# Picking each expert's 64 tokens: drawing the highest of three sequences early, in partition quarters, and merging them with the fourth

## The chip, the cores and the metric

The kernel runs on one core of a Trainium2 chip. The metric is the device time of one execution in microseconds (us). A core has five engines that run their own instruction lists and wait for each other through semaphores: TensorE (PE, matrix products and transposes, into PSUM), VectorE (DVE), ScalarE (ACT), GpSimd (POOL) and SyncE (SP, which here only issues DMAs).

## What is computed

The reference is a decoder of two layers on x of 4 sequences x 256 tokens x 128. Layer 0 is local attention, then self and cross attention, then a mixture of 16 experts; layer 1 is a recurrence, cross attention and a second mixture. The change concerns the choice of tokens in layer 0's mixture:

```
logits = xn @ router_weight.T + router_bias      # 1024 tokens x 16 experts
probs = jax.nn.softmax(logits, axis=-1)
_, idx = jax.lax.top_k(logits.T, top_k)          # top_k = 64 tokens of 1024, for each expert
xe = xn[idx]
...
output = jnp.zeros((n_tokens, d)).at[flat_idx].add(contrib)
```

Each expert takes the 64 tokens with its highest logits out of all four sequences; of equal logits the earlier token goes first.

## The kernel before

**The attention pipeline.** Layer 0's attention is `attention_pipeline` with 12 jobs: 4 local ones, then self and cross attention of each sequence in turn. Job n begins its core work at slot 16n, and every engine walks through the slots 0 to 249 in order and does in each what falls into it: a unit of row maxima (PE scores, DVE `nmax` at L1093), one head of scores and exponentials (PE L866, ACT L974), a quarter of the products with V (PE L907), and the job's end steps: transpose (L820), division (`y`, L1036 to L1043), output product (L772), residual sum and statistics (`z`, L1052 to L1060), 1/std on POOL (L753), and norm (L1069 writes `m.x[1]`, the tokens for the experts, with semaphore `xs_ready`; L1073 writes `m.x[2]`). The last job, number 11, is the cross attention of sequence 3: its 16 heads are slots 214 to 229, its division is in DVE's slot 237, its sum in slot 241, its norm in slot 243. Waits only follow data: a slot has no fixed length, and an engine may be slots ahead of another.

**Side work.** `expert_choice` hangs its own steps into the slots (`sync`, `gpsimd`, `tensor`, `scalar`, `vector`, each called at the head of a slot) and continues after the last slot (`sync_on`, `gpsimd_on`, ...). A side step that uses the shared PSUM bank M1 (bank 7) has its turn in the list `part.uses`, and waits until the use before it has been read.

**The choice.** Before the change PE transposes the tokens of sequences 0 and 1 in slot 230 and of sequence 2 in slot 234 (L1266), ACT multiplies them by the norm weight (L1375), PE makes the logits [16 x 1024] in three groups (L1272), ACT adds the bias (L1380); the last group (sequence 3) follows after the last slot. Then DVE takes the eight highest of all 1024 columns (MAX8, L1436) and overwrites them with a constant (MATCH_REPLACE8, L1438), eight times, marks the places taken (L1440), counts them along the row (a scan, L1441), and so has `posb`, the slot number of each token in each expert or 0 (L1442). PE turns `posb` (L1304), DVE copies it (L1448) and compares it with 1 to 64 for each of 8 token tiles (L1451), which makes the one-hot matrices `onehot`; PE gathers the tokens with them (L1312, 48 products of 512 columns), and the experts follow. SP writes `posb` to DRAM and reads it back 16 times, spread over partitions, for the scatter (L1214, L1217). POOL splits the normed tokens `xn` into three bf16 terms (L1247 to L1250). `keep_warm` runs 18 products that nobody reads (L504) on PE before `posb` is there.

Of the kernel before, what the change touches and what calls it, by code (L numbers as in the profile page):

```python
# [14 lines left out]
BF16 = mybir.dt.bfloat16  # L15
# [9 lines left out]
P = 128  # L25
# [452 lines left out]
GROUPS = ((0, 512), (512, 768), (768, 1024))  # L478
S_ROUTER, S_NORM_COL, S_OPEN = 140, 226, 230
# [657 lines left out]
def expert_choice(nc, m, dram, ctx, rec):  # L1137


    part = Core()  # L1140
# [12 lines left out]
    logits = m.xres[0:E0, :, :].rearrange("p t d -> p (t d)")  # L1153
    work = m.x[0][0:E0, :, :].rearrange("p t d -> p (t d)")
    top8 = sb("top8", [E0, 8])
    ones = sb("ones", [E0, TOK], BF16)
    posb = sb("posb", [E0, TOK], BF16)
    taken = m.xT[0][0:E0, 0:TOK // 2].bitcast(BF16)
    count = m.xT[0][0:E0, TOK // 2:TOK].bitcast(BF16)
# [14 lines left out]
    wr = sb("wr", [P, E0])  # L1174
    rb = sb("rb", [E0, 1])
# [16 lines left out]
        "h_mm", "h_in", "h_act", "y_mm", "ygl_ready", "out_mm")]  # L1192
    var_ready, rms_ready, ex_in, rounds, turning = sem("var_ready"), sem("rms_ready"), sem("ex_in"), sem("rounds"), sem("turning")
    x2, x3 = m.x[2], m.x[0]
    out_rows = lambda i: (B[2], B[3], B[6], B[7])[i // 2][:, (i % 2) * D:(i % 2 + 1) * D]
    part.uses = [(S_NORM_COL, "norm_col", 0), (S_OPEN, "xs", 0)]

    def sync(sp, slot):
        if slot == S_ROUTER:
            sp.dma_start(wr[:, :], dram["routerT"]).then_inc(r_in, 16)  # L1200
            sp.dma_start(rb[:, :], dram["router_b"]).then_inc(r_in, 16)
            sp.dma_start(b1[:, :, :], dram["fc1b"]).then_inc(w_in, 16)
            for half in range(2):
                src = dram["fc2b"].rearrange("(r o) d -> o r d", o=2)[half:half + 1, :, :]
                sp.dma_start(b2[64 * half:64 * half + 64, :, :], src.to_broadcast([64, PAIRS, D])).then_inc(w_in, 16)

    def sync_on(sp):
        sp.wait_ge(part.pv_done, 12 * BATCH)
        sp.dma_start(fc2, dram["fc2T"]).then_inc(fc2_in, 16)
        sp.wait_ge(r_in, 32)  # L1210
# [3 lines left out]
        sp.dma_start(pos_rows, posb[:, :]).then_inc(pos_out, 16)  # L1214
        sp.wait_ge(pos_out, 16)
# [10 lines left out]
    def gpsimd(pool, slot):  # L1226
        if slot != S_OPEN:
            return
        g = nc.gpsimd
        link = chain(pool, pchain, pool_count)  # L1230
# [9 lines left out]
        pool.wait_ge(const, 3)  # L1240

    def gpsimd_on(pool):
        g = nc.gpsimd
        link = chain(pool, pchain, pool_count)
        pool.wait_ge(xnT_mm, 2)
        pool.wait_ge(xn_ready, 2)
# [5 lines left out]
        pool.wait_ge(lg_in, 3)  # L1252
# [11 lines left out]
    def turned(pe, bank, first, tiles, done):  # L1264
        for i in tiles:
# [3 lines left out]
    def routed(pe, bank, k):  # L1269
        pe.wait_ge(xnT_in, k + 1)  # L1270
        lo, hi = GROUPS[k]
        nc.tensor.matmul(bank[0:E0, 0:hi - lo], wr[:, :], xnT[:, lo:hi], start=True, stop=True).then_inc(lg_mm, 1)  # L1272

    def tensor(pe, slot):
# [4 lines left out]
        if slot == S_OPEN:  # L1279
            pe.wait_ge(part.m1_read, part.m1_no["xs", 0])  # L1280
            pe.wait_ge(part.xs_ready, 2)
            turned(pe, M1, 0, range(0, 4), part.m1_full)
        if slot == S_OPEN + 4:
            pe.wait_ge(part.xs_ready, 3)
            turned(pe, B[1], 4, range(4, 6), xnT_mm)
        if slot == S_OPEN + 7:
            pe.wait_ge(r_in, 32)
            routed(pe, B[0], 0)
        if slot == S_OPEN + 9:
            routed(pe, B[2], 1)  # L1290

    def tensor_on(pe):
        t = nc.tensor
        pe.wait_ge(part.xs_ready, 4)
        turned(pe, B[3], 6, range(6, 8), xnT_mm)
        routed(pe, B[1], 2)
        pe.wait_ge(lg_in, 3)
        for i in range(TILES):
            t.transpose(B[4][:, i * E0:(i + 1) * E0], logits[:, i * P:(i + 1) * P], m.ident[0:E0, 0:E0]).then_inc(lgT_mm, 1)
        pe.wait_ge(rounds, CAP // 8 - 1)  # L1300
# [72 lines left out]
    def weighed_by_norm(act, bank, k):  # L1373
        lo, hi = GROUPS[k]
        return nc.scalar.activation(xnT[:, lo:hi], bank[:, 0:hi - lo], ACT.Copy, scale=norm_col[:, :])  # L1375

    def with_bias(act, bank, k):
        act.wait_ge(lg_mm, k + 1)
        lo, hi = GROUPS[k]
        nc.scalar.activation(logits[:, lo:hi], bank[0:E0, 0:hi - lo], ACT.Identity, bias=rb[:, :]).then_inc(lg_in, 1)  # L1380

    def scalar(act, slot):
# [5 lines left out]
        if slot == S_OPEN + 1:  # L1388
            act.wait_ge(part.m1_full, part.m1_no["xs", 0] + 1)
            weighed_by_norm(act, M1, 0).then_inc(part.m1_read, 1)  # L1390
            act.wait_ge(part.m1_read, part.m1_no["xs", 0] + 1)
            s.sem_inc(xnT_in, 1)
        if slot == S_OPEN + 5:
            act.wait_ge(xnT_mm, 1)
            weighed_by_norm(act, B[1], 1).then_inc(xnT_in, 1)
# [878 lines left out]
```

## Time and profile before

| what | value |
|---|---|
| three timed runs | 572.04, 574.46 (median), 580.11 us |
| the profiled execution | 571.62 us |
| its span in the trace | 569.9 us |
| mean granted TensorE clock | 0.955 of full speed |
| busy: PE, DVE, ACT, POOL | 470.7, 372.7, 223.3, 186.6 us |

The span runs from the first to the last instruction in the trace; 1.72 us of the execution lie outside it. Rows name a line of the kernel, an engine and an operation, output<-input with their sizes (partitions x columns), and a count. An idle time in square brackets is that of the engine just before the row, with what ended it.

### The profile page before, as it was taken

What the parts mean: (1) busy time and instruction counts of PE and PEld (TensorE: products, weight loads), DVE (VectorE), ACT (ScalarE), POOL (GpSimd) and SP (SyncE); (2) the same over time, 40 slices, a digit from 0 to 9 for tenths busy, and PEclk for the clock granted to TensorE, in tenths of its full rate; (3) what the DMA queues carried; (4) which work ended last, traced back from release to release, by engine and by line L of the source; (5) the groups of instructions that cost most, each with busy time, mean ns of one, the idle gap of its engine ahead of it and who ended that gap; (6) DMA issues with size and microseconds to landing.
All of it is one profiled execution on the core that took longest, in us unless ns stands there. A gap on an engine that the chain in (4) does not pass through costs nothing. (4 is left out here: it accounts for less than half of the span.)

```text
span 569.9 us, 10425 instructions
## 1 busy us (share of the span) xinstructions
PE 470.7 (83%) x3785; PEld 232.4 (41%) x3832; DVE 372.7 (65%) x868; ACT 223.3 (39%) x451; POOL 186.6 (33%) x310
## 2 busy tenths in 40 slices
PE   3899899988979889885069998697799888999993
PEld 2445444433334333332026986254233333444441
DVE  7555766877677677823996474854478784466574
ACT  1313444445754656673002122332114667624220
POOL 7752639467344471333200005720542100000000
PEclk9999999989998999998579999899699999999998
DMA  7230103054441220007013040000321100250700
GB/s 240 72 96 12 49 2 104 21 178 138 144 106 49 58 56 3 2 3 294 0 39 112 2 168 2 0 1 1 85 56 37 48 3 3 67 157 2 222 18 19
DMA packets 26900, 38.03 MB, mean 67 GB/s; under 512 B 3649, under 2 KB 19521, under 8 KB 26465
## 3 DMA queue, kind: packets, MB, share of 16 engines
q1 hardware_dynamic: 26848, 37.36, 21.8%
q8 instruction: 31, 0.51, 0.4%
q14 instruction: 21, 0.16, 0.1%
HBM read 23.91 MB, written 0.59 MB: 43 GB/s over the span
## 5 line engine op out<-in xcount | busy, mean ns | idle before, releaser
L1093 DVE TENSOR_REDUCE nmax<-bank 128x2 f32<-128x512 f32 (+2 forms) x240 | 144.4, 624 | 79.6 <-PE bank L862 37.9
L974 ACT ACTIVATE arena<-bank 128x512 f32<-128x512 f32 (+2 forms) x256 | 130.9, 526 | 122.6 <-PE bank L866 84.7
L862 PE MATMUL bank<-arena 62*128 62x256 bf16 (+2 forms) x512 | 86.0, 257 | 11.8 <-DVE nmax L1093 5.0
L504 PE MATMUL bank<-causal_qk,identb 128*128 128x512 bf16 x232 | 71.1, 402 | 26.1 <-DVE moe_top L1436 16.0
L866 PE MATMUL bank<-arena 64*128 64x256 bf16 (+2 forms) x512 | 85.8, 256 | 2.2 <-ACT arena L974 1.5
L907 PE MATMUL bank<-arena 128*32 128x256 f32 (+4 forms) x1088 | 73.0, 347 | 9.3 <-POOL arena L729 2.8
L862 PEld LDWEIGHTS bank<-arena 62*128 62x128 bf16 x512 | 29.8, 94 | 77.5 <-issue 46.6
L504 PEld LDWEIGHTS bank<-causal_qk,identb 128*128 128x128 bf16 x275 | 23.8, 104 | 55.7 <-DVE moe_top L1436 15.7
L729 POOL TENSOR_SCALAR_AFFINE_SELECT arena<-arena 128x256 f32<-128x256 f32 x64 | 25.6, 410 | 48.8 <-ACT arena L974 48.0
L866 PEld LDWEIGHTS bank<-arena 64*128 64x128 bf16 x512 | 30.3, 94 | 16.6 <-ACT arena L974 6.5
L907 PEld LDWEIGHTS bank<-arena 128*32 128x32 f32 x1088 | 21.4, 109 | 34.2 <-issue 19.1
L688 POOL TENSOR_TENSOR arena<-qk,arena 128x512 bf16<-128x512 f32 x15 | 17.4, 1157 | 52.2 <-ACT arena L936 52.2
L518 POOL TENSOR_SCALAR veps<-mv 128x2 f32<-128x2 f32 x8 | 1.5, 193 | 91.0 <-DVE mv L1541 73.8
L2085 ACT ACTIVATE arena<-bank 128x512 f32<-128x512 f32 x24 | 14.3, 597 | 40.6 <-PE bank L2067 40.6
L2095 DVE TENSOR_TENSOR arena<-bank,arena 128x512 f32<-128x512 f32 x24 | 16.5, 689 | 16.4 <-ACT arena L2085 16.1
L2072 PE MATMUL bank<-arena,fcw 128*128 128x512 f32 x48 | 24.5, 594 | 0.4 <-DVE arena L2101 0.4
L2066 PE MATMUL bank<-xT,fcw 128*128 128x512 f32 x48 | 24.7, 596 | 0.0
L2067 PE MATMUL bank<-xT,fcw 128*128 128x512 f32 x48 | 24.5, 592 | 0.0
L751 POOL TENSOR_SCALAR veps<-mv 128x2 f32<-128x2 f32 x12 | 2.7, 225 | 64.1 <-DVE mv L1060 63.8
L784 PE MATMUL bank<-xT,h 128*128 128x256 f32 x32 | 11.8, 453 | 11.6 <-DVE h L400 9.9
L2137 POOL TENSOR_TENSOR rstd<-veps,eps 128x4 f32<-128x4 f32 x2 | 2.0, 1008 | 55.3 <-DVE veps L2178 55.3
L928 ACT ACTIVATE qk<-bank,qs_cols 128x256 f32<-128x256 f32 x16 | 7.5, 470 | 29.9 <-PE bank L785 29.9
(296 smaller groups left out, 813.5 us busy)
## 6 DMA issues: line engine op xcount, KB each, us to landing
arena<-arena SPq DMA_DIRECT2D x96, 128.0 KB, 2.4
fcw<-in_fc1T SPq DMA_DIRECT2D x16, 256.0 KB, 3.3
arena<-in_fc2T SPq DMA_DIRECT2D x1, 4096.0 KB, 12.5
arena<-comb_rows SPq DMA_DIRECT2D x16, 256.0 KB, 4.3
fcw<-in_last SPq DMA_DIRECT2D x1, 2304.0 KB, 8.3
arena<-pos_rows SPq DMA_DIRECT2D x16, 128.0 KB, 3.0
arena<-comb_rows SPq DMA_DIRECT2D x16, 128.0 KB, 4.3
w<-in_w SPq DMA_DIRECT2D x1, 1216.0 KB, 6.1
```

Source lines behind the costliest of these rows:

```text
L504: nc.tensor.matmul(bank[:, :], m.identb[:, :], m.causal_qk[:, 0:4, :], start=True, stop=True)
L688: g.tensor_tensor(parts[:, 4], src, parts[:, 0], ALU.subtract).then_inc(split, 1)
L729: g.affine_select(out=part, in_=part, compare_op=ALU.is_ge, fill=0.0, base=0, pattern=[[0, 2], [1, P]], channel_multiplier=-1).then_inc(ke ...
L862: mins = t.matmul(mout[:, i, :], stack_rows(m, nm, h0 + i, 0, MAX_ROWS)[:, qt * P:(qt + 1) * P], stack_rows(m, nm, h0 + i, 1, MAX_ROWS)[:, ...
L866: sins = t.matmul(sout[i], stack_rows(m, nh, h, 1, SCORE_ROWS)[:, i * P:(i + 1) * P], stack_rows(m, nh, h, 0, SCORE_ROWS)[:, spans[i][0]:s ...
L907: ins = t.matmul(PV[n % len(PV)][32 * i:32 * i + 32, lo + a:lo + b], m.vaug[n % 4][:, k, h, :], m.prob[h % 8][:, o0 + a - q0:o0 + b - q0], ...
L974: s.activation(m.prob[h % 8][:, 0:w], score_bank(n, h)[:, 0:w], ACT.Exp).then_inc(exps, 1)
L1093: v.tensor_reduce(m.nmax[n % 2][:, qt, h0:h0 + nh], MX[c % NMX][:, 0:nh * (k1 - k0)].rearrange("p (h k) -> p h k", h=nh), AX.X, ALU.max, n ...
L2066: t.matmul(B[k][:, :], self.w1[:, f * P:(f + 1) * P], xT, start=True, stop=True)
L2067: t.matmul(B[k + 1][:, :], self.w3[:, f * P:(f + 1) * P], xT, start=True, stop=True).then_inc(self.hg_mm, 1)
L2072: self.nc.tensor.matmul(self.acc[c][:, :], self.w2[:, f, :], self.hid[u % 2], start=(f == 0), stop=(f == HT - 1)).then_inc(self.o_mm, 1)
L2095: v.tensor_tensor(self.sil[u % 2], self.m.bank[2 * (u % 2) + 1][:, :], self.sil[u % 2], ALU.mult).then_inc(self.gs_in, 1)
```

## The change

The logits of the four sequences lie one under another: sequence b in partitions 32b to 32b+15, 256 columns each. They are made by four products, each with the router's weights padded by zeros to 32 columns. The transposes and logits of sequences 0 and 1 are moved to slots 196 and 199, those of sequence 2 to slots 216 and 219, all in bank M1; the norm column goes from slot 226 to 186. In its slots 222 to 229 DVE draws, in eight rounds, the 64 highest of each of the first three sequences at once (96 partitions x 256 columns). In slot 230 it copies the three lists side by side ([16 x 192]); the 64 highest of these are drawn in eight rounds: two in slot 238, one in 239, two in 242, three after the last slot. When the logits of sequence 3 are there, they are copied beside that list ([16 x 320]), and eight rounds give the 64th highest value of each expert. DVE then compares all logits ([128 x 256]) with it, "greater" and "equal", and counts both by a scan; two small products on PE with 0/1 matrices (`before_it`, `of_expert`, made on POOL in slot 230) give each partition the counts of the sequences before it; from these come `posb`, now [128 x 256]. The product that makes `xn` moves from DVE (L1420) to POOL, as one instruction after the last norm. `keep_warm` starts after the fourth of the last eight rounds instead of the seventh of before.

```diff
+QUARTER = P // BATCH
+EARLY = QUARTER * (BATCH - 1)
+S_ROUTER, S_NORM_COL, S_OPEN = 140, 186, 226
+S_TURN, S_ROUTED = ((196, 0, 4), (216, 4, 6)), ((199, (0, 1)), (219, (2,)))
+S_DRAW, S_GATHER, S_MERGE = 222, 230, (238, 238, 239, 242, 242)
...
+    logits = flat[:, 0:SEQ]
+    pooled = flat[0:E0, SEQ:2 * SEQ + CAP]
+    three = flat[0:E0, 2 * SEQ + CAP:3 * SEQ]
+    lists = flat[0:EARLY, 3 * SEQ + CAP:3 * SEQ + 2 * CAP]
+    highest = flat[0:E0, 3 * SEQ + 2 * CAP:3 * SEQ + 3 * CAP]
...
+            sp.wait_ge(padded, 2)
+            sp.dma_start(wr[:, 0:E0], dram["routerT"]).then_inc(r_in, 16)
+            for b in range(BATCH):
+                sp.dma_start(rb[QUARTER * b:QUARTER * b + E0, :], dram["router_b"]).then_inc(r_in, 16)
...
-        sp.dma_start(pos_rows, posb[:, :]).then_inc(pos_out, 16)
-        sp.wait_ge(pos_out, 16)
+        for b in range(BATCH):
+            sp.dma_start(pos_rows[:, b * SEQ:(b + 1) * SEQ], posb[QUARTER * b:QUARTER * b + E0, :]).then_inc(pos_out, 16)
+        sp.wait_ge(pos_out, 16 * BATCH)
...
+        g.memset(fact[:, :], 0.0).then_inc(const, 1)
+        for matrix, quarters in ((before_it, range(1, BATCH)), (of_expert, range(1 - BATCH, BATCH))):
+            link(g.memset(matrix[:, :], 0.0))
+            for q in quarters:
+                link(g.affine_select(out=matrix[:, :], in_=matrix[:, :], compare_op=ALU.not_equal, fill=1.0,
+                                     base=QUARTER * q, pattern=[[-1, P]], channel_multiplier=1))
+        g.sem_inc(const, 1)
+        pool.wait_ge(const, 5)
...
+        pool.wait_ge(part.xs_ready, BATCH)
+        pool.wait_ge(part.pv_done, 9 * BATCH)
+        link(g.tensor_tensor(xn, m.x[1][:, :, :], row(m, "moe_norm").unsqueeze(1).broadcast_to([P, TILES, D]), ALU.mult))
+        pool.wait_ge(xnT_mm, 1)
...
+        for k, (at, lo, hi) in enumerate(S_TURN):
+            if slot == at:
+                pe.wait_ge(part.m1_read, part.m1_no["xs", k])
+                pe.wait_ge(part.xs_ready, hi // QT)
+                turned(M1, lo, hi, part.m1_full)
+        for k, (at, sequences) in enumerate(S_ROUTED):
+            if slot == at:
+                pe.wait_ge(r_in, 16 + 16 * BATCH)
+                pe.wait_ge(part.m1_read, part.m1_no["routed", k])
+                routed(M1, sequences, part.m1_full)
...
+        pe.wait_ge(drawn, 1)
         keep_warm(nc, m, B[7], F_ROUTE)
+        pe.wait_ge(counted, 1)
+        pe.wait_ge(const, 5)
+        t.matmul(B[2][:, 0:2], before_it[:, :], ranks[:, :, SEQ - 1], start=True, stop=False, skip_group_check=True)
+        t.matmul(B[2][:, 1:2], of_expert[:, :], ranks[:, 0, SEQ - 1:SEQ], start=False, stop=True, skip_group_check=True).then_inc(count_mm, 1)
...
+        for k, (at, lo, hi) in enumerate(S_TURN):
+            if slot == at + 1:
+                act.wait_ge(part.m1_full, part.m1_no["xs", k] + 1)
+                weighed_by_norm(M1, lo, hi).then_inc(part.m1_read, 1)
+        for k, (at, sequences) in enumerate(S_ROUTED):
+            if slot == at + 1:
+                act.wait_ge(r_in, 16 + 16 * BATCH)
+                act.wait_ge(part.m1_full, part.m1_no["routed", k] + 1)
+                with_bias(M1, sequences).then_inc(part.m1_read, 1)
...
+    def draw(link, source, out, spent, i):
+        v = nc.vector
+        eight = out[:, 8 * i:8 * i + 8]
+        link(v.max(eight, spent if i else source))
+        if i < CAP // 8 - 1:
+            link(v.match_replace(out=spent, in_to_replace=eight, in_values=spent if i else source, imm_value=TAKEN))
...
+        if slot == S_DRAW:
+            dve.wait_ge(part.m1_read, part.m1_no["routed", 1] + 1)
+        if S_DRAW <= slot < S_DRAW + CAP // 8:
+            draw(link, logits[0:EARLY, :], lists, work, slot - S_DRAW)
+        if slot == S_GATHER:
+            for b in range(BATCH - 1):
+                link(v.tensor_copy(three[:, CAP * b:CAP * (b + 1)], lists[QUARTER * b:QUARTER * b + E0, :]))
+        for i, at in enumerate(S_MERGE):
+            if slot == at:
+                draw(link, three, pooled[:, 0:CAP], three, i)
...
+        for i in range(len(S_MERGE), CAP // 8):
+            draw(link, three, pooled[:, 0:CAP], three, i)
+        dve.wait_ge(lg_in, 1)
+        link(v.tensor_copy(pooled[:, CAP:CAP + SEQ], logits[EARLY:EARLY + E0, :]))
...
+            draw(link, pooled, highest, pooled, i)
+            if i == CAP // 16 - 1:
+                v.sem_inc(drawn, 1)
+        dve.wait_ge(const, 5)
+        for b in range(BATCH):
+            link(v.tensor_copy(fact[QUARTER * b:QUARTER * b + E0, 0:1], highest[:, CAP - 1:CAP]))
+        for k, op in enumerate((ALU.is_gt, ALU.is_equal)):
+            link(v.tensor_scalar(compared[:, k, :], logits, fact[:, 0:1], None, op))
+        for k in range(2):
+            link(v.tensor_tensor_scan(ranks[:, k, :], ones[:, :], compared[:, k, :], 0.0, ALU.mult, ALU.add))
+        v.sem_inc(counted, 1)
+        dve.wait_ge(count_mm, 1)
+        link(v.tensor_copy(fact[:, 1:3], B[2][:, 0:2]))
+        for k in range(2):
+            link(v.scalar_tensor_tensor(out=placed[:, k, :], in0=ranks[:, k, :], scalar=fact[:, 1 + k:2 + k], in1=compared[:, k, :],
+                                        op0=ALU.add, op1=ALU.mult))
+        link(v.tensor_scalar(kept, placed[:, 1, :], float(CAP), None, ALU.is_le))
+        link(v.tensor_tensor(kept, kept, placed[:, 1, :], ALU.mult))
+        v.tensor_tensor(posb[:, :], placed[:, 0, :], kept, ALU.add).then_inc(pos_ready, 1)
```

## Rows read from the trace of the kernel before

**Rows 1.** The waits from 240 to 330 us: who waited for whom, total us, times, longest.

```profile
ACT moe_gate L1408 <- DVE moe_lgT L1446: 24.8, 1, 24.8
POOL veps L518 <- DVE mv L1060: 16.0, 1, 16.0
```

**Rows 2.** DVE's timeline, 228 to 312 us: start us, us, what.

```profile
259.26 0.36 DVE L1036 RECIPROCAL rden<-bank 128x32 f32<-128x32 f32 x1 [7.46 <-PE bank L820]
...
262.53 0.42 DVE L1052 TENSOR_TENSOR z<-bank,xres 128x256 f32<-128x256 f32 x1 [1.93 <-PE bank L772]
...
266.25 0.60 DVE L1073 TENSOR_SCALAR x<-z,mv,rstd 128x128 f32<-128x128 f32 x2
...
269.21 1.22 DVE L1436 MAX8 moe_top<-xres 16x8 f32<-16x1024 f32 x1 [2.03 <-ACT xres L1380]
...
292.71 0.68 DVE L1442 TENSOR_TENSOR moe_posb<-xT 16x1024 bf16<-16x1024 bf16 x1
...
294.16 9.17 DVE L1451 TENSOR_TENSOR arena<-moe_iota_s,moe_posT 128x1024 bf16<-128x1024 bf16 x8
```

**Rows 3.** PE's timeline, 254 to 308 us.

```profile
255.97 0.66 PE L1266 MATMUL bank<-ident,x 128*128 128x128 f32 x4
...
259.15 1.03 PE L1272 MATMUL bank<-xT,moe_wr 128*16 128x512 f32 x2
...
286.23 5.72 PE L504 MATMUL bank<-causal_qk,identb 128*128 128x512 bf16 x17 [15.97 <-DVE moe_top L1436]
293.44 0.35 PE L1304 MATMUL bank<-identb,moe_posb 16*128 16x16 bf16 x8 [1.49 <-DVE moe_posb L1442]
295.53 12.21 PE L1312 MATMUL bank<-arena 128*128 128x512 bf16 x47 [1.73 <-DVE arena L1451]
```

**Rows 4.** DVE's instruction groups by form, 268 to 295 us: busy us, mean ns | idle.

```profile
L1436 DVE MAX8 moe_top<-x 16x8 f32<-16x1024 f32 x7 | 8.5, 1216 | 0.2
L1438 DVE MATCH_REPLACE8 x<-moe_top,x 16x1024 f32<-16x1024 f32 x7 | 8.4, 1196 | 0.0
L1441 DVE TENSOR_TENSOR_SCAN xT<-moe_ones,xT 16x1024 bf16<-16x1024 bf16 x1 | 2.3, 2278 | 0.0
...
L1440 DVE TENSOR_SCALAR xT<-x 16x1024 bf16<-16x1024 f32 x1 | 0.7, 682 | 0.0
L1442 DVE TENSOR_TENSOR moe_posb<-xT 16x1024 bf16<-16x1024 bf16 x1 | 0.7, 678 | 0.0
L1438 DVE MATCH_VALUE_LOAD x<-moe_top,x 16x8 f32 x7 | 0.6, 79 | 0.2
```

**Rows 5.** The shortest group that MAX8 has in the kernel, and the scan of 256 and the three-operand operation of 512 columns, by form.

```profile
L1787 DVE SCALAR_TENSOR_TENSOR arena<-bank,cols,hid 128x512 f32<-128x512 f32 x8 | 6.0, 751 | 10.4 <-ACT hid L1712 10.3
...
L1762 DVE TENSOR_TENSOR_SCAN arena<-arena,cols 128x256 f32<-128x256 f32 x4 | 2.8, 738 | 0.1
...
L1924 DVE MAX8 top_top<-top_lg 128x8 f32<-128x8 f32 x8 | 1.3, 167 | 0.2
```

**Rows 6.** Timelines of all engines at 170 us, of DVE at 240 and of POOL at 268 us.

```profile
170.26 1.16 POOL L696 TENSOR_TENSOR rem<-qk,arena 128x512 f32<-128x512 f32 x1
...
170.77 0.68 DVE L1082 CAST nml<-nmax 128x32 bf16<-128x32 f32 x1
...
240.19 0.18 DVE L1082 CAST nml<-nmax 128x32 bf16<-128x32 f32 x1
...
268.46 2.12 POOL L1248 TENSOR_TENSOR x<-arena 128x1024 f32<-128x1024 f32 x1
```

**Rows 7.** Busy time 228 to 246 us (PE, PEld, DVE, ACT, POOL; PE clock, DMA share, GB/s).

```profile
228.00:246.00 18.00, 15.04 (x170) 6.17 (x172) 13.12 (x29) 11.26 (x25) 8.13 (x22) 1.00 0.01 4
```

**Rows 8.** The waits of SP's queue from 150 to 215 us.

```profile
SPq L649 <- ACT arena L936: 20.7, 3, 8.6
```

**Rows 9.** Stretches of 1 us, with the granted PE clock third from the end.

```profile
296.00:297.00 1.00, 1.00 (x6) 0.45 (x5) 1.00 (x2) 0.00 (x0) 0.00 (x0) 0.93 0.23 90
...
300.00:301.00 1.00, 1.00 (x5) 0.44 (x4) 1.00 (x2) 0.00 (x0) 0.00 (x0) 0.86 0.56 201
```

More of the change, by code:

```diff
@@ L1152, in expert_choice @@
     xnT = m.xT[0]
[L1153 to L1159, printed above, removed]
+    flat = m.hid[:, :, :].rearrange("p a c -> p (a c)")
+    logits = flat[:, 0:SEQ]
[3 more added lines that the diff above has]
+    highest = flat[0:E0, 3 * SEQ + 2 * CAP:3 * SEQ + 3 * CAP]
+    work = m.qk32[0][0:EARLY, 0:SEQ]
+    ones = sb("ones", [P, SEQ], BF16)
+    posb = sb("posb", [P, SEQ], BF16)
+    compared = m.xT[0][:, 0:SEQ].bitcast(BF16).rearrange("p (k t) -> p k t", k=2)
+    ranks = m.xT[0][:, SEQ:2 * SEQ].bitcast(BF16).rearrange("p (k t) -> p k t", k=2)
+    placed = m.xT[0][:, 2 * SEQ:3 * SEQ].bitcast(BF16).rearrange("p (k t) -> p k t", k=2)
+    kept = m.xT[0][:, 3 * SEQ:3 * SEQ + SEQ // 2].bitcast(BF16)
+    fact = sb("fact", [P, 3])
+    before_it = sb("before_it", [P, P], BF16)
+    of_expert = sb("of_expert", [P, P], BF16)
     posT = sb("posT", [P, TILES, E0], BF16)
@@ L1251, in gpsimd_on @@
         pool.wait_ge(xnl_ready, 1)
-        pool.wait_ge(lg_in, 3)
+        pool.wait_ge(lg_in, 1)
+        pool.wait_ge(part.x1_ready, 2 * BATCH)
         pool.wait_ge(fc2_in, 16)
@@ L1262, in gpsimd_on, with turned, routed @@
         rec.gpsimd_on(pool)
-    def turned(pe, bank, first, tiles, done):
-        for i in tiles:
+    def turned(bank, first, last, done):
+        for i in range(first, last):
             ins = nc.tensor.transpose(bank[:, (i - first) * P:(i - first + 1) * P], m.x[1][:, i, :], m.ident[:, :])
         ins.then_inc(done, 1)
[L1269 to L1272, printed above, removed]
+    def routed(bank, sequences, done):
+        for b in sequences:
+            ins = nc.tensor.matmul(bank[QUARTER * b:QUARTER * (b + 1), 0:SEQ], wr[:, :], xnT[:, b * SEQ:(b + 1) * SEQ], start=True, stop=True)
+        ins.then_inc(done, 1)
     def tensor(pe, slot):
@@ L1278, in tensor @@
             t.transpose(M1[:, 0:P], row(m, "moe_norm"), m.ident[:, :]).then_inc(part.m1_full, 1)
[L1279 to L1288, printed above, removed]
@@ L1292, in tensor_on @@
     def tensor_on(pe):
         t = nc.tensor
[L1294 to L1300, printed above, removed]
+        pe.wait_ge(part.xs_ready, BATCH)
+        turned(B[3], TILES - QT, TILES, xnT_mm)
+        pe.wait_ge(xnT_in, 1)
@@ L1302, in tensor_on @@
         pe.wait_ge(pos_ready, 1)
-        for i in range(TILES):
-            t.transpose(B[5][:, i * E0 // 2:(i + 1) * E0 // 2].bitcast(BF16), posb[:, i * P:(i + 1) * P],
-                        m.identb[0:E0, 0:E0]).then_inc(posT_mm, 1)
+        for q in range(QT):
+            t.transpose(B[5][:, q * P // 2:(q + 1) * P // 2].bitcast(BF16), posb[:, q * P:(q + 1) * P],
+                        m.identb[:, :]).then_inc(posT_mm, 1)
         pe.wait_ge(xnl_ready, 1)
@@ L1371, in tensor_on, with weighed_by_norm, with_bias @@
         rec.tensor_on(pe)
[L1373 to L1380, printed above, removed]
+    def weighed_by_norm(bank, lo, hi):
+        return nc.scalar.activation(xnT[:, lo * P:hi * P], bank[:, 0:(hi - lo) * P], ACT.Copy, scale=norm_col[:, :])
+    def with_bias(bank, sequences):
+        lanes = slice(QUARTER * sequences[0], QUARTER * (sequences[-1] + 1))
+        return nc.scalar.activation(logits[lanes, :], bank[lanes, 0:SEQ], ACT.Identity, bias=rb[lanes, :])
     def scalar(act, slot):
```

84 lines of the change are left out of this document (30 added, 54 removed).

## Prediction, written before the changed kernel was run

> **What bounds the kernel now.** I read the waits around 240 to 330 us first, then the timelines of the engines there. The chain of waits that ended last begins only at 397 us, so it says nothing of this place. ACT waits 24.8 us for the logits' exponentials [rows 1], because DVE alone works: from 269.21 to 294.16 it goes without a pause through eight rounds, the marking, the scan and the product, and only then starts the one-hot matrices [rows 2]. PE idles 15.97 us in it [rows 3]. Ahead of it the order is: sum `z` at 262.53 (waits for PE's output product), norm, transposes and logits of sequence 3, first MAX8 at 269.21 after 2.03 us for ACT's bias [rows 2]. Nothing after it is tied to a time of its own: `posb` at 293.39 (292.71 + 0.68) releases PE, DVE and SP's round trip alike, and the gather products run from 295.53 for 12.21 us [rows 3]. So what DVE saves between 269.2 and 293.4 comes off the end nearly one for one, unless PE's clock takes some of it back.
>
> **What is removed.** One round is 1216 + 79 + 1196 = 2491 ns of instructions [rows 4]; the eight rounds, marking, scan and product take 293.39 - 269.21 = 24.18 us, of which the rounds are 20.47 (289.68 is what is left ahead of 682 + 2278 + 678 ns and their gaps), so 69 ns of a round are gaps.
>
> **What the last eight rounds cost.** They work on 320 columns. MAX8 takes 167 ns for 8 columns [rows 5] and 1216 for 1024, so 1.03 ns a column: 0.49 us for 320. MATCH_REPLACE8 at the same slope: 0.47 (1196 less 704 columns). A round is 0.49 + 0.08 + 0.46 + 0.07 = 1.09 us; seven of them and a last MAX8 are 8.2 us. That the partitions don't matter is seen in MAX8's 128 partitions at 167 ns, near the fixed part of the 16-partition form.
>
> **The rest of the new chain on DVE.** Four copies of one column, 0.20 us each with its wait (bounds 0.1 and 0.25): 0.8. Two comparisons of 256 columns with a scalar from memory: the marking took 682 for 1024 [rows 4], so about 0.35 (0.28 to 0.42), 0.75 with gaps. Two scans of 256: 738 ns each [rows 5], 1.55. Two products on PE and back: no row has such a pair. The eight small transposes took 0.35 and started 0.05 after `posb` [rows 3]; I take 0.5 (0.35 to 0.8), and 0.2 for reading the counts. Two three-operand operations: 751 for 512 columns [rows 5], so 0.46 each, 1.0 together (0.7 to 1.1). The last three, from the product's 678 for 1024 [rows 4], are 0.22 + 0.28 + 0.28 with gaps 0.85. Sum 5.65, bounds 4.7 to 6.5. With the rounds: 13.8 us from the copied logits to `posb`, where 24.18 stand now. The turn of `posb`, the maximum and `posT` are the same work in another layout (two transposes of 128 partitions for eight small ones); I cost them at nothing, at most 0.3.
>
> **The early draws.** On 96 x 256 a round is 0.42 + 0.08 + 0.40 + 0.07 = 0.97 us, together 7.3, and 0.6 for the three copies. DVE stood idle for 7.46 us up to the division of job 11 at 259.26 [rows 2], from 251.80 that is, and what it did just before, the first part of the `xn` product, goes. From about 251 (an estimate, with ACT's bias of slot 220 ahead of it) the draws end at 258.9, so they fit with 0.4 us to spare. Without that cover each us over costs one.
>
> **The merges.** On 192 columns a round is 0.35 + 0.08 + 0.34 + 0.07 = 0.84 us. The three of slots 238 and 239 follow the division, which ends at 260.6 (262.53 - 1.93): 2.5 us to 263.1, where `z` stood ready at 262.53 [rows 2]. Cost 0.6 us, on the path: the logits come at 269.8 instead of 269.2. The two of slot 242 (1.7) lie in the wait for POOL's 1/std. The last three, 2.1 us, lie in the 2.03 us in which DVE waits for sequence 3's logits.
>
> **POOL and the port.** The `xn` product on 1024 columns now starts when the last L1069 is done, with DVE's two L1073 still under way; its like took 2.12 us [rows 6]. The rows show what such a meeting does: DVE's cast of 32 columns, 0.18 us when POOL is idle, took 0.68 at 170.77 and ended at 171.45, as POOL's product did at 171.42 [rows 6]. MAX8 and MATCH_REPLACE8 are not held: all eight are 1216 and 1196 ns [rows 4], and POOL's product ran from 268.46. So I expect: POOL takes its turn between the two L1073; the second ends some 2.1 us late (267.2 + 2.1); three merges (2.1) end at 271.4; the copy of sequence 3's logits then meets POOL's next product and gets through at about 272.8 instead of 270.1 (269.8 + 0.3). The other end is 270.6, if DVE comes first at L1073 and the copy waits only for the rest of a shorter POOL cast. I take 272.8, as that cast did.
>
> The Trainium skill (SBUF — State Buffer, Who interferes with whom) says the same of the pair of ports which the two engines share: whoever issues first keeps it for its whole instruction; copies and tensor-scalar forms ask for it, an instruction with one input outside those modes does not. It speaks against moving `xn` to POOL; by it the time is the forecast below, without it 2.2 us less.
>
> **What moves into the attention loop.** PE's six transposes and the logits of three sequences leave slots 230 to 239, where they lay beside ACT's and DVE's steps, and go to slots 196 to 219. The four transposes took 0.66 and 512 columns of logits 1.03 [rows 3]: 2.5 us of PE altogether, and some 2 us of ACT, most of it into a stretch in which PE is busy 15.04 of 18 us, DVE 13.12 and ACT 11.26 [rows 7]. If the idle 2.96 us absorb them, 0; if PE is always the last, 2.6. I take 1.2, near the middle, since no engine is full there. The semaphores are old by then (sequence 2's norm is over before slot 216). The norm column is moved unchanged.
>
> **POOL's and SP's other steps.** POOL builds its matrices between 248 and 264, where it waits 16.0 us [rows 1], and nobody needs them before 279; cost nothing, though a delay of its 1/std would be paid in full. SP waits in slot 140 for two memsets and issues three more small DMAs, with the stack transfers behind it. In those SP waits for ACT anyhow, 20.7 us in three times [rows 8]; against waits of that size three issues cost nothing. The four writes of `posb` instead of one are 1 us more of SP; the first columns are needed after nine us of one-hot matrices, so nothing.
>
> **PE's clock.** At 1.2 GHz a product of 512 columns lasts twice as long. In the gather stage the clock stood at half from the end of the slice 296-297 to early in 300-301 [rows 9], some 3.3 us, about 5 after the reader-less products had ended at 291.95 [rows 3]. Now these start at about 278.4 (272.8 + 1.2 + four rounds) and end by 284.3; the gather starts 2.14 us after `posb`, as now, at about 289.9. The gap is 5.6 us, where it was 3.6 (295.53 - 291.95), so the clock is likely down when the gather starts. What a cold start costs: 48 products less 1.65 us of half clock are 10.56 us, 0.22 each, so the 17 reader-less ones would be 3.7 us and took 5.72 [rows 3], 2 us lost instead of 1.65. Cost 0.3.
>
> **Sum.** `posb`: 272.8 + 13.8 + 1.2 = 287.8 instead of 293.39, so 5.6 earlier, less 0.3: 5.3 us. The 0.6 of the merges stands in the 269.8. Against the profiled execution's 571.62: 566.3. That execution is the fastest of four; the median of all four (571.62, 572.04, 574.46, 580.11) is 573.25, or 1.6 above it, so I forecast **567.9 us**.
>
> **The rivals.**
> - A, everything fits better: POOL holds nothing (2.2), the loop absorbs the moved work (1.2) and the clock stays up in the gather (1.9 with the 0.3): 562.6. For it: DVE's instructions are queued ahead of POOL's. Against: the cast of rows 6. Chance 0.2.
> - B, the other end: the loop pays 2.6, the chain 6.5 instead of 5.65, and the early draws run 1 us over the division's time: 3.2 us less gained, 571.1. Chance 0.2.
> - C, slower than before: the loop is in lockstep. PE waits in its four new places for ACT's reads, with the scores and maxima of both running jobs queued behind it, and DVE and ACT wait for those; if each place costs over 1.6 us ((5.3 + 1.2) / 4), the change loses. At 2.5 us each it is 10 less the 1.2 counted: 576.7. Against: the bank was read slots before each of these places, and ACT is busy 11.26 of 18 us [rows 7]. Chance 0.05.
> - D, the port: what is held isn't one instruction each but also the comparisons and `z`; the reverse of A: another 2 us, 569.9. POOL is through with its five instructions by 276, before the comparisons. Chance 0.05.
>
> The forecast itself (565 to 570) has 0.5. Two per cent (11.5 us) are about what a measurement of this kernel can tell from no change: faster by over 2% needs all of A and a low median, 0.1; slower by over 2% needs C at full price, 0.02; within 2%, 0.88. The range, 561.5 to 572.5, takes in A and B.
>
> **What the changed profile would show.** MAX8 on 16x320 of 0.48 to 0.50 us, eight times; draws over before the last division; `z` 0.6 us later against the division; the second L1073 near 2 us late, ending with POOL's product; 13 to 15 us from the copy to `posb`; the slots 196 to 220 longer by 0 to 2.6; the clock's half-speed stretch at the gather's start. The prediction is wrong if DVE's draws start so late that they pass the division's time, if the four column copies or the trip to PE cost over 1 us more than stated, or if the clock stays down through the gather (48 products, up to 8 us more).

## The result: 572.4 us, 3.3 us less by the ratio, where 5.3 to 6.9 were forecast

| | before | changed |
|---|---|---|
| median of 13 runs each | 574.75 us (571.52 to 580.11) | 572.43 us (568.88 to 577.35) |
| ratio of the runs | | 0.9943, 95% interval 0.9918 to 0.9968 |
| profiled execution, time / span | 571.62 / 569.9 us | 577.35 / 575.5 us |

The medians are 2.3 us apart; the ratio, which weighs all 13 runs of each, says 3.3 us less, between 1.8 and 4.7. Within 2% was given a chance of 0.88. The forecast, 567.9, asked for 5.35 us less than the median that it started from, and for 6.85 less than this one. In the ratios of the experiments below, runs more than 1.5% above the fastest of their kernel are left out, which concerns one of six and two of twelve in the two kernels whose only addition is products ahead of the gather. The profiled execution of the changed kernel is the longest of its 13, so whole spans can't be compared. What can are stretches of it that begin and end with the same instruction. First DVE's timeline:

```profile
227.71 0.36 DVE L1039 RECIPROCAL rden<-bank 128x32 f32<-128x32 f32 x1 [0.41 <-PE bank L823]
243.48 0.35 DVE L1039 RECIPROCAL rden<-bank 128x32 f32<-128x32 f32 x1
257.34 0.36 DVE L1039 RECIPROCAL rden<-bank 128x32 f32<-128x32 f32 x1 [4.60 <-PE bank L823]
...
265.65 0.62 DVE L1465 COPY hid<-hid 16x64 f32<-16x64 f32 x3
266.86 0.36 DVE L1039 RECIPROCAL rden<-bank 128x32 f32<-128x32 f32 x1 [0.60 <-PE bank L823]
270.83 0.42 DVE L1055 TENSOR_TENSOR z<-bank,xres 128x256 f32<-128x256 f32 x1
274.08 0.60 DVE L1072 TENSOR_SCALAR x<-z,mv,rstd 128x128 f32<-128x128 f32 x2 [0.39 <-DVE hid L1454]
274.60 2.64 DVE L1076 TENSOR_SCALAR x<-z,mv,rstd 128x128 f32<-128x128 f32 x2
279.19 1.42 DVE L1476 COPY hid<-hid 16x256 f32<-16x256 f32 x1
280.64 0.48 DVE L1452 MAX8 hid<-hid 16x8 f32<-16x320 f32 x1
294.00 0.29 DVE L1496 TENSOR_TENSOR moe_posb<-xT 128x256 bf16<-128x256 bf16 x1
294.98 9.17 DVE L1508 TENSOR_TENSOR arena<-moe_iota_s,moe_posT 128x1024 bf16<-128x1024 bf16 x8
311.38 0.69 DVE L1521 TENSOR_TENSOR hid<-bank,moe_b 128x512 f32<-128x512 f32 x1 [4.96 <-PE bank L1391]
```

The reader is to take differences of starts. The divisions (L1039) close attention jobs 8 to 11, counted from 0: 15.77 us from job 8's to job 9's, 13.86 to job 10's, 9.52 to job 11's. In the kernel before, the same divisions are 14.66, 13.13 and 9.51 apart; its first three (the fourth is in [rows 2]):

```profile
221.96 0.36 DVE L1036 RECIPROCAL rden<-bank 128x32 f32<-128x32 f32 x1 [0.41 <-PE bank L820]
236.62 0.35 DVE L1036 RECIPROCAL rden<-bank 128x32 f32<-128x32 f32 x1
249.75 0.36 DVE L1036 RECIPROCAL rden<-bank 128x32 f32<-128x32 f32 x1 [3.87 <-PE bank L820]
```

From the last division to `z` it is now 3.97 (before: 262.53 - 259.26 = 3.27 [rows 2]); from `z` to the end of `posb` 23.46 (before 30.86, 262.53 to 293.39). The eight early draws stood between 258.37 and 265.61 and were through 1.25 us before the division that follows them.

DVE's groups by form from 280 to 295 us (busy us, mean ns | idle), which answer to [rows 4]:

```profile
L1452 DVE MAX8 hid<-hid 16x8 f32<-16x320 f32 x8 | 3.9, 482 | 0.4
L1454 DVE MATCH_REPLACE8 hid<-hid 16x320 f32<-16x320 f32 x7 | 3.2, 464 | 0.0
L1476 DVE COPY hid<-hid 16x256 f32<-16x256 f32 x1 | 1.4, 1421 | 0.0
L1487 DVE TENSOR_TENSOR_SCAN xT<-moe_ones,xT 128x256 bf16<-128x256 bf16 x2 | 1.4, 691 | 0.1
...
L1492 DVE SCALAR_TENSOR_TENSOR xT<-xT,moe_fact 128x256 bf16<-128x256 bf16 x2 | 1.0, 484 | 0.1
L1485 DVE TENSOR_SCALAR xT<-hid,moe_fact 128x256 bf16<-128x256 f32 x2 | 0.7, 353 | 0.1
L1483 DVE COPY moe_fact<-hid 16x1 f32<-16x1 f32 x4 | 0.6, 144 | 0.1
...
L1490 DVE COPY moe_fact<-bank 128x2 f32<-128x2 f32 x1 | 0.2, 159 | 0.4 <-PE bank L1335 0.4
```

The new chain runs from the copy's end at 280.61 to `posb`'s end at 294.29: 13.68 us, 13.8 forecast. Next POOL and PE, timelines of the same stretch:

```profile
274.81 2.34 POOL L1275 TENSOR_TENSOR arena<-x,rows 128x1024 f32<-128x1024 f32 x1 [0.83 <-POOL rstd L756]
...
278.34 2.12 POOL L1278 TENSOR_TENSOR x<-arena 128x1024 f32<-128x1024 f32 x1
```

```profile
269.42 1.19 PE L775 MATMUL bank<-w,yT 128*128 128x128 f32 x4 [0.60 <-ACTq L956]
...
285.49 5.67 PE L507 MATMUL bank<-causal_qk,identb 128*128 128x512 bf16 x17 [7.19 <-DVEq L1480]
291.94 0.18 PE L1334 MATMUL bank<-xT,moe_before_it 128*128 128x2 bf16 x1 [0.77 <-DVEq L1488]
294.35 0.28 PE L1338 MATMUL bank<-identb,moe_posb 128*128 128x128 bf16 x2 [2.21 <-DVE moe_posb L1496]
296.35 12.03 PE L1346 MATMUL bank<-arena 128*128 128x512 bf16 x47 [1.72 <-DVE arena L1508]
```

DVE's L1076 ends at 277.24 and POOL's product (L1275) at 277.15; DVE's copy ends at 280.61 and POOL's L1278 at 280.46. Each time DVE gets through when POOL does. The merges' MAX8 and MATCH_REPLACE8 between them, with POOL at work, take 0.34 and 0.33 us, as they do with POOL idle (0.35 and 0.33). Last, two of the 1 us windows, with PE's granted clock third from the end, which answer to [rows 9]:

```profile
296.00:297.00 1.00, 0.65 (x2) 0.29 (x3) 1.00 (x2) 0.00 (x0) 0.00 (x0) 0.52 0.07 17
...
299.00:300.00 1.00, 1.00 (x5) 0.37 (x4) 1.00 (x2) 0.00 (x0) 0.00 (x0) 0.78 0.51 189
```

The clock stands at half when the gather starts and is back during 299 to 300; in the kernel before it fell only in 296 to 297, after the gather had begun.

**The ledger.** From job 8's division to the first one-hot matrix the kernel before takes 72.20 us, the changed one 67.27: 4.93 less, as loop +1.11 and +0.73, merges +0.70, `z` to `posb` -7.40, the rest -0.07. From the one-hot matrices to the first bias sum (L1521), the gather, before took 16.57 (PE as in [rows 3], 12.21) and the changed kernel 16.40 in these two profiles. Outside, the profile of after is longer: by 5.4 us from the start to job 6's division (192.51 for 187.09) and by 4.8 from the bias sum to layer 1's first division (147.60 for 142.77). The experiments show below how far the kernel before does the same by itself.

### The profile page after: what moved, and what is told of

It is laid out like the page before. It is cut to its first block and busy times, and to the rows that moved or that the text cites. A ratio compares the mean times of both kernels' runs of the same rounds, so it can differ in the third digit from the quotient of the medians.

```text
span 575.5 us, 10505 instructions
## 1 busy us (share of the span) xinstructions
PE 480.7 (84%) x3778; PEld 235.1 (41%) x3824; DVE 376.9 (66%) x923; ACT 223.1 (39%) x451; POOL 191.9 (33%) x326
## 5 line engine op out<-in xcount | busy, mean ns | idle before, releaser
L507 PE MATMUL bank<-causal_qk,identb 128*128 128x512 bf16 x233 | 74.4, 417 | 17.3 <-DVEq L1480 7.2
```

Of the source, the lines that this page charges most:

```text
L507: nc.tensor.matmul(bank[:, :], m.identb[:, :], m.causal_qk[:, 0:4, :], start=True, stop=True)
```

## The experiments

Ten runs were made: the kernel before once more, and eight others, one of them twice. None leaves work out. "Loop" below is the sum of the two distances between divisions, jobs 8 to 10: 27.79 us before, 29.63 changed.

Several expectations go by a longer stretch, from job 6's division to the experts' first bias sum: 123.64 us before, 118.87 changed. It came to 116.66 with the late POOL product (as its theory has it), 120.07 with the work issued twice, 119.44 with the work moved later and 131.29 with the draws at the end, where the theories had 120.5 to 121, 118.2 to 118.6 and 126 to 129. But the stretch takes in jobs 6 to 8, which vary from 34.1 to 36.7 us, and the gather, so the readings below go by the shorter distances.

**Take POOL's product away from DVE's norm and copy.** POOL waits for DVE's copy of the last logits before it starts `xn`; on the changed kernel.

```
+    copied = sem("copied")
+        pool.wait_ge(copied, 1)
         link(g.tensor_tensor(xn, m.x[1][:, :, :], row(m, "moe_norm")...
...
         link(v.tensor_copy(pooled[:, CAP:CAP + SEQ], logits[EARLY:EARLY + E0, :]))
+        v.sem_inc(copied, 1)
```

> I read every run by one stretch, from the start of the division of job 6 (the seventh RECIPROCAL of rden) to DVE's first bias sum of the experts; it is 123.64 us in the profile before and 118.87 in the profile after, and leaves out the differences of PE's clock ahead of it and behind it. Here POOL starts its xn product only when DVE has copied sequence 3's logits. Theory (POOL's product holds DVE's second L1076 and then the copy for a whole instruction each): the two L1076 take 0.6 us instead of 2.64, the copy 0.3 instead of 1.42, and the stretch is 116.6 to 117.1. Rival (the copy and the norm are slow by themselves, across partitions or in this layout): both keep their length and the stretch stays at 118.9.

DVE's timeline of this run, then POOL's:

```profile
268.19 0.60 DVE L1076 TENSOR_SCALAR x<-z,mv,rstd 128x128 f32<-128x128 f32 x2
...
271.25 0.29 DVE L1478 COPY hid<-hid 16x256 f32<-16x256 f32 x1 [0.56 <-ACT hid L1414]
```

```profile
271.77 2.34 POOL L1277 TENSOR_TENSOR arena<-x,rows 128x1024 f32<-128x1024 f32 x1 [4.18 <-DVEq L1479]
```

The same two instructions fall from 2.64 to 0.60 us and from 1.42 to 0.29, and `z` to `posb` from 23.46 to 21.04: 2.42 us, where the prediction had 2.2. POOL's product, which waits 4.18 us for it, delays nothing up to the one-hot matrices. 566.19 us in its one run. Timed against the kernel before in five rounds, the same code:

> The kernel in which POOL waits for the copy, timed. Its stretch from job 8's division to posb was 2.4 us shorter than after's. Theory (that is kept): the ratio to the kernel before is 0.988 to 0.992, where the change alone has 0.9943. Rival (a change of PE's clock takes it back): 0.994 or more.

569.43 us median of 6 (566.48 to 571.94), ratio 0.9878, interval 0.9832 to 0.9925. That the two instructions waited for POOL is shown, and so is the price in the rows. The ratio is 0.0065 below the changed kernel's, which is 3.7 us, and just below the 0.988 that the theory gave as its lower end; the two intervals overlap by 0.0007, so the price in the whole time is less sure than the 2.42 us in the rows.

**Issue the moved work of PE and ACT twice,** to size it: each of the moved transposes and logit products, and each of ACT's reads of them (the first copies into a scratch tile), once more in its slot.

```
+                for i in range(lo, hi):
+                    t.transpose(M1[:, (i - lo) * P:...], m.x[1][:, i, :], m.ident[:, :])
                 turned(M1, lo, hi, part.m1_full)
...
+                s.activation(again[...], M1[:, 0:(hi - lo) * P], ACT.Copy, scale=norm_col[:, :])
                 weighed_by_norm(M1, lo, hi).then_inc(part.m1_read, 1)
```

> PE's transposes and logit products of slots 196, 199, 216 and 219 and ACT's reads of them are issued twice. Theory (what is moved into the loop is paid nearly in full, by the busy time of PE): from the division of job 8 to that of job 10 the time grows by 1.8 us again, as it did from 27.79 to 29.63 with the first copy, and the stretch is 120.5 to 121. Rival (the loop has idle time that takes it, and the 1.8 us came from the order of waits): it grows by under 0.8.

Its divisions, DVE's timeline:

```profile
220.22 0.36 DVE L1039 RECIPROCAL rden<-bank 128x32 f32<-128x32 f32 x1 [0.43 <-PE bank L823]
...
251.73 0.36 DVE L1039 RECIPROCAL rden<-bank 128x32 f32<-128x32 f32 x1 [5.58 <-PE bank L823]
```

The loop takes 31.51 us: a second copy of the work costs 1.88, and the first had cost 1.84. The busy times over the loop (PE, PEld, DVE, ACT, POOL) show how much of it the engines' idle time took up, in the kernel before, the changed one and this one:

```profile
221.96:249.75 27.79, 23.50 (x253) 9.43 (x256) 16.24 (x37) 18.14 (x37) 9.93 (x26) 1.00 0.01 3
```

```profile
227.71:257.34 29.63, 25.71 (x265) 10.17 (x268) 16.42 (x36) 19.95 (x41) 11.40 (x35) 1.00 0.01 3
```

```profile
220.22:251.73 31.51, 27.90 (x280) 11.33 (x279) 16.41 (x36) 21.22 (x45) 12.01 (x37) 1.00 0.01 3
```

PE has 2.21 us more work and then 2.19 more; its idle time falls only from 4.29 to 3.92 and to 3.61. So five sixths of PE's added work is paid for. PE's and ACT's parts were doubled together, so the run doesn't tell their shares. 571.50 us in one run.

**Move the first part of it later,** where it might lie under DVE's idle time ahead of job 10's division.

```
-    S_TURN, S_ROUTED = ((196, 0, 4), (216, 4, 6)), ((199, (0, 1)), (219, (2,)))
+    S_TURN, S_ROUTED = ((210, 0, 4), (216, 4, 6)), ((213, (0, 1)), (219, (2,)))
```

> The transposes and logits of sequences 0 and 1 go from slots 196 and 199 to 210 and 213, behind the last row maxima. Theory (they cost 1.1 us in slots in which PE feeds both maxima and scores): the 1.1 between the divisions of jobs 8 and 9 goes, 0.4 to 0.8 comes back between 9 and 10, and the stretch is 118.2 to 118.6. Rival (the work costs its PE time wherever it stands): 118.9 as after.

```profile
221.64 0.36 DVE L1039 RECIPROCAL rden<-bank 128x32 f32<-128x32 f32 x1 [0.41 <-PE bank L823]
...
251.25 0.36 DVE L1039 RECIPROCAL rden<-bank 128x32 f32<-128x32 f32 x1 [4.79 <-PE bank L823]
```

Jobs 8 to 9 are back at 14.65 us, and jobs 9 to 10 went to 14.96: the loop takes 29.61 against 29.63. My theory (1.1 goes, and 0.4 to 0.8 comes back) fell, since 1.10 came back; the rival (it costs the same wherever it stands in this loop) held at this one other place. 570.22 us in one run.

**Draw everything after the last slot.** The eight draws, the three copies and all eight merges follow the attention loop.

```
-    S_DRAW, S_GATHER, S_MERGE = 222, 230, (238, 238, 239, 242, 242)
+    S_DRAW, S_GATHER, S_MERGE = 222, 230, ()
...
+        for i in range(CAP // 8):
+            draw(link, logits[0:EARLY, :], lists, work, i)
```

> The draws of the three sequences, the three copies and all merges stand behind the last slot. Theory (the early draws are hidden altogether and the merges cost 0.7): 7.9 us of draws and copies and 4.1 of merges come onto the path, less 0.7 and less the 2 us in which DVE waited for sequence 3, and some held time goes too: the stretch is 126 to 129, slower than before the change. Rival (the draws are not hidden, they delay the last job): the stretch grows by under 5 us.

DVE's timeline:

```profile
263.07 0.36 DVE L1039 RECIPROCAL rden<-bank 128x32 f32<-128x32 f32 x1 [8.64 <-PE bank L823]
...
266.34 0.42 DVE L1055 TENSOR_TENSOR z<-bank,xres 128x256 f32<-128x256 f32 x1 [1.93 <-PE bank L775]
...
300.37 0.29 DVE L1495 TENSOR_TENSOR moe_posb<-xT 128x256 bf16<-128x256 bf16 x1
```

The idle time of 8.64 us that the draws fill is to be seen ahead of the division, and the division to the next is 9.52 with draws and without: they are hidden. `z` to `posb` grows by 10.86 us to 34.32, and the last division to `z` falls by 0.70 to 3.27, the number of the kernel before: 0.70 is the price of the merges ahead of `z`. The 10.86 are the 7.9 of draws and copies and the 4.1 of five merges, less the 1.14 by which the copy is no longer held; the 2 us that the expectation took off for DVE's wait for sequence 3 aren't there, since the changed kernel's DVE goes from its merges to the copy without a pause. Unhidden, the change costs more than it saves: 34.32 from `z` to `posb` is 3.46 more than before, with the loop's 1.84 on top. 583.09 us in one run, beside 575.36 of the kernel before on the same chip, one run too.

**Give POOL the whole `xn` product in the kernel before,** to see the port alone.

```
-            weighed_rows(0, 6).then_inc(xn_ready, 1)
-        weighed_rows(6, 8).then_inc(xn_ready, 1)
+        link(g.tensor_tensor(xn, m.x[1][:, :, :], row(m, "moe_norm")..., ALU.mult))
```

> One part of the change alone, in the kernel before: POOL makes the xn product as one instruction after the last norm, DVE no longer does. Theory (POOL's product holds DVE's second L1073 for its own length): the two L1073 take 2.6 us instead of 0.60, but they end at about 268.9 on before's time scale, ahead of the first MAX8 at 269.21, so from the division of job 11 to the end of posb it stays at 34.13 us within 0.1: the hold costs nothing where DVE has a pause behind it. Rival (the hold needs the new layout or the merges): the two L1073 take 0.6.

DVE's timeline, then POOL's, and last the part of the product that DVE makes there in the kernel before:

```profile
266.75 2.64 DVE L1073 TENSOR_SCALAR x<-z,mv,rstd 128x128 f32<-128x128 f32 x2
269.72 1.22 DVE L1434 MAX8 moe_top<-xres 16x8 f32<-16x1024 f32 x1 [0.32 <-ACT xres L1383]
```

```profile
266.97 2.34 POOL L1247 TENSOR_TENSOR arena<-x,rows 128x1024 f32<-128x1024 f32 x1 [0.77 <-POOL rstd L753]
```

```profile
266.76 0.42 DVE L1420 TENSOR_TENSOR arena<-x,rows 128x256 f32<-128x256 f32 x1
```

L1073 is held here too, 2.64 for 0.60 us, and DVE's pause ahead of MAX8, in which it waits for ACT's logits, takes the hold up: the pause falls from 2.03 [rows 2] to 0.32, that is by the 2.04 us of the hold less the third of a microsecond of the product that DVE doesn't make. MAX8 starts 2.97 us after L1073, where it was 2.96, and last division to `posb` is 34.13 us, as in the kernel before (3.27 + 30.86). In the changed kernel the last three merges fill that pause, and so the hold costs its full price. 572.11 us in one run, beside 576.17, the median of 11 of before on that chip; one run doesn't tell them apart.

**The kernel before, profiled again,** to see what two profiles of one program differ by.

> The kernel before, unchanged, for a second profile of it. In the five profiles with the changed code the time from the experts' first bias sum to the first division of layer 1 is 143.6 to 147.6 us, in the one profile before it is 142.77, with the same instructions. Theory (this is the phase of PE's clock, which differs from run to run): this profile gives 144 to 148, and the division of job 6 comes at another time than 187.09. Rival (the change loses 1 to 5 us there by its timing): 142.8 again.

PE's timeline:

```profile
288.48 6.23 PE L504 MATMUL bank<-causal_qk,identb 128*128 128x512 bf16 x18 [15.58 <-DVE moe_top L1436]
...
298.18 10.52 PE L1312 MATMUL bank<-arena 128*128 128x512 bf16 x48 [1.74 <-DVE arena L1451]
```

577.38 us, 5.8 above the first profile. From job 8's division to the one-hot matrices the distances are those of the first profile within 0.01 us each. The differences lie elsewhere: start to job 6's division 190.08 us instead of 187.09, the gather 14.89 instead of 16.57, and from the bias sum to layer 1's first division 147.58 instead of 142.77. The windows of the first 60 us (busy time of PE, PEld, DVE, ACT and POOL, then PE's granted clock, DMA share, GB/s) show what goes with the first of these; in this order the first profile of before, this one, and the changed kernel's:

```profile
0.00:60.00 60.00, 47.24 (x321) 23.95 (x325) 37.13 (x89) 15.57 (x39) 34.05 (x64) 1.00 0.33 100
```

```profile
0.00:60.00 60.00, 47.94 (x295) 23.89 (x295) 35.59 (x85) 14.71 (x37) 31.49 (x61) 0.97 0.34 100
```

```profile
0.00:60.00 60.00, 47.65 (x279) 23.39 (x283) 34.17 (x84) 14.40 (x35) 30.37 (x60) 0.94 0.34 99
```

The clock is 1.00, 0.97 and 0.94, in a stretch whose code the change doesn't touch, and job 6's division comes at 187.09, 190.08 and 192.51. Changed code has 1.00 there too, in five of its profiles, such as the run with the late POOL product (job 6 at 187.26) and that with the work issued twice (185.66). From the bias sum to layer 1 the twelve profiles lie between 142.7 and 148.0, and both of these ends are of kernels with the old routing. So the 5.4 and 4.8 us can't be laid to the change.

**Keep PE at work up to the gather.** In the changed kernel six products without a reader after the counting products and five after the turn of `posb`.

```
     ....then_inc(count_mm, 1)
+        keep_warm(nc, m, B[7], 6)
...
     m.identb[:, :]).then_inc(posT_mm, 1)
+        keep_warm(nc, m, B[7], 5)
```

> The change with one thing added: 6 products that nobody reads behind the two counting products and 5 behind the transposes of posb (POOL isn't moved). In the changed kernel's profile the time from the first one-hot matrix to the first bias sum of the experts is 16.40 us (16.4 to 17.8 in six profiles with this code and no fillers), in the two profiles of the kernel before 16.57 and 14.89. Theory (the longer pause ahead of the gather makes the half clock in it certain, where before it comes and goes, and this takes back part of the gain): 14.9 here, and the ratio to before falls from 0.9943 to 0.990 to 0.992. Rival (the clock of the gather isn't what is missing): 14.9, but the ratio stays at 0.993 to 0.996.

569.89 us median of 6 (565.27 to 574.31), ratio 0.9885, interval 0.983 to 0.994. The gather takes 14.89 us, as where the clock is full; after had 16.40. The stretch ahead of it is unchanged (`z` to `posb` 23.45). The ratio is lower than both the theory (0.990 to 0.992) and the rival say, and the gather's 1.5 us (16.40 less 14.89) are 0.0026 of the time, not 0.0058; but the interval overlaps the changed kernel's, so the rest may be chance. The same five products in the kernel before:

> The kernel before with 5 products that nobody reads behind the transposes of posb. Theory: the gather always runs at full clock, 14.9 us from the first one-hot matrix to the first bias sum, and since about half of the runs before have that anyhow, the ratio to the kernel before is 0.997 to 0.999. Rival (nearly all runs before have the half clock): 0.996 or less; or (nearly none has it): 1.000.

573.61 us median of 12, ratio 0.9949, interval 0.9916 to 0.9982; the 48 gather products take 10.52 us. This is more than the 0.997 to 0.999 expected, though 0.997 lies inside; over all twelve runs the ratio of the means is 0.9962. It speaks for the rival, that nearly all runs of the kernel before have the half clock in the gather; of the three profiles without added products (this kernel's two and that with POOL's `xn`) two have it. The 1.7 us that it can be worth there are 0.3%, so either nearly every run has it or more is gained at a place I haven't found. This stays open.

**All of it together:** the late POOL product, four and eight products in the pauses around the last output product, and the eleven ahead of the gather.

```
+        if slot == 237:
+            keep_warm(nc, m, B[0], 4)
+        if slot == 241:
+            keep_warm(nc, m, B[0], 8)
```

> As the kernel in which POOL waits, with products that nobody reads in PE's pauses: 4 in slot 237, 8 in slot 241, 6 behind the two counting products, 5 behind the transposes of posb. Theory (PE's clock falls in the pause of the last job's end and again between keep_warm and the gather, and this costs time): the two transposes and logits of sequence 3 take 0.4 and 0.6 us instead of 0.69 and 1.06, the gather runs 10.5 us, together 1.5 to 2.5 us less than the kernel without them. Rival (the clock falls anyhow, or the fillers delay what follows): no less, or up to 1 us more.

PE's timeline:

```profile
265.83 0.68 PE L775 MATMUL bank<-w,yT 128*128 128x128 f32 x4 [0.60 <-ACTq L956]
...
271.15 0.44 PE L1299 MATMUL bank<-ident,x 128*128 128x128 f32 x2 [2.90 <-DVE x L1072]
272.15 1.06 PE L1304 MATMUL bank<-xT,moe_wr 128*32 128x256 f32 x2 [0.56 <-ACT xT L1416]
...
290.10 10.52 PE L1354 MATMUL bank<-arena 128*128 128x512 bf16 x48 [0.64 <-DVE arena L1517]
```

566.80 us median of 6 (564.30 to 571.22), ratio 0.9842, interval 0.9794 to 0.9891: the lowest ratio of all, though its interval overlaps those of the two halves. L775 is back at 0.68 us (1.19 in after), but `z` doesn't gain by it: last division to `z` is 3.96 as in after, since DVE's merges end it. The two transposes fall from 0.69 to 0.44, the two logit products stay at 1.06 where 0.6 was expected, and `z` to `posb` is 20.80, 0.24 less than with the late product alone. The gather's 14.89 is the rest.

## Why the prediction was wrong

The mechanism on DVE was right, and within 2% was the likeliest verdict. None of the three signs of being wrong that the prediction named came up: the draws passed no division, the copies and the trip to PE cost less than stated, and the clock came back in the gather. Two terms failed: the work moved into the attention loop, taken at 1.2 us and measured at 1.84, and the step from the profiled execution to the median, taken at 1.6 and 3.1 with more runs. What PE's clock cost is open.

- **The chain from the copied logits to `posb`**: 13.8 us forecast, 13.68 measured. The rounds 8.2 forecast, 8.27 measured (280.61 to 288.88). The slope of 1.03 ns a column from two widths of MAX8 held for both instructions. The four column copies took 0.68 instead of 0.8, the way to PE and back 0.35 instead of 0.5.
- **The early draws**: hidden, as stated, with 0.60 us of idle time left (0.4 forecast); the run with all draws at the end shows the 8.64 us that they fill.
- **The port**: 2.2 forecast, 2.42 measured. It held exactly the two instructions named, and Rival D (the comparisons and `z` too) doesn't occur: the comparisons take 353 ns each, and run some 6 us after POOL's fifth instruction ended. The rule of the Trainium skill (SBUF — State Buffer, Who interferes with whom), that whoever issues first keeps the shared pair of ports for its whole instruction, is borne out: the scalar form and the copy waited for POOL's (2.64 for 0.60, 1.42 for 0.29), MAX8 didn't (0.34 us for 192 columns beside POOL, 0.35 without).
- **What moves into the attention loop**: this step failed. I took 1.2, "near the middle, since no engine is full there". The rows give 1.84, twice the work costs twice (31.51 against 29.63), and another place for the first part cost the same. PE's busy time in the loop grew by 2.21 us, and only 0.37 of it came out of its idle time. So the 2.96 us that PE idles of 18 [rows 7] are not free for such work. My explanation, argued only, is that these gaps are PE's own waits in a ring of PE, DVE and ACT steps, and a step put in pushes the ring on instead of filling a gap.
- **The merges**: 0.6 forecast, 0.70 measured.
- **PE's clock**: not settled. I took 0.3, since the profile of before had the half clock in the gather already. It doesn't in every run: the three profiles with the old routing and no added products take 16.57, 14.89 and 16.57 us from one-hot to bias sum (mean 16.0), the six of the changed kernel and its variants without added products ahead of the gather 16.40, 17.76, 16.37, 16.95, 17.14 and 17.56 (mean 17.0). From the reader-less products' end to the gather PE has 4.5 to 5.8 us in these six (291.16 to 296.35 in the changed kernel) with 0.6 us of short products in it, and 3.5 to 3.6 in the three. The half clock came in all six, and filling the pause took it away. The means are 1.0 apart, but that is from few profiles, and five added products in the kernel before speak against it: if nearly all of its runs have the half clock, the term is 17.0 - 16.57, under 0.5.
- **The median**: also a failed term. I added 1.6 us from the profiled execution to the median of four runs. With thirteen runs the median of before is 3.1 above it (574.75 - 571.62). The sum's 5.3 us less would have been 569.5 on that scale, and 567.9 claims 6.85.

The prediction had `posb` 5.6 us earlier. Loop +0.64, merges +0.1, port +0.2 and chain -0.1 leave 4.8, and the ledger shows 4.93, just outside the measured 1.8 to 4.7. With 0.3 to 1.0 in the gather it is 4.6 to 3.9 us less, inside it. The 0.6 to 1.3 us from there to the ratio's 3.3 have no row; they are within its noise. Rival A is out (the port holds, and the loop absorbs 0.4 of PE's 2.2 us). B named the loop's upper bound, 2.6, and its 571.1 is nearest to the result, but two of its three parts (the chain at 6.5, the draws over time) didn't occur, so that its number is near is luck. C, the lockstep, would need 1.6 us a place; it was 0.46 (1.84 / 4).

Open: whether the head and the part from bias sum to layer 1 differ by the change at all, since they differ by 3.0 and 4.8 us between two profiles of the kernel before; and what the moved norm column costs, which can't be seen in jobs 6 to 8 (34.1 to 36.7 us in all variants).

## What to carry to other kernels

A chain of narrow instructions can be costed from two widths of the same instruction to a few per cent. Idle time read off a busy share was not free in a loop in which several engines wait for each other (five sixths of PE's added work was paid for): double the work for one run, or count it in full. Where POOL is given a long tensor product, list DVE's copies and scalar forms in that time, as each was held to its end here; the hold costs nothing where DVE has a pause behind it, and one semaphore that starts POOL after them took back 2.4 us. And before shortening a pause-free stretch on one engine, see what the other's clock does with the shape of the pauses that are left.

## What I had not expected

- The hold is per instruction and to the end of POOL's: two norm instructions took 2.64 us in the changed kernel and in the kernel before with POOL's product, to the same digits, and the copy 1.42 instead of 0.29.
- The distances between divisions 8 to 11 repeat to 0.02 us from profile to profile of like code, while the stretch ahead of job 6 varies from 185.7 to 192.5 us. Seven profiles with a granted clock of 1.00 over the first 60 us have 185.7 to 187.6, three with 0.94 have 188.0 to 192.5. A ratio within 1% of this kernel is a matter of many runs.
- Eleven products that nobody reads, some 2.7 us of PE's time in its pauses, shorten the gather from 12.03 us to 10.52 in one profile of each.
